# Mamba loop on one core: the order of ScalarE's queue within a tile, and one semaphore count for each square

## The chip, the cores and the metric

The kernel runs on one core of a Trainium2 chip. The metric is device time in microseconds (us) from one launch. Before the change three runs took 1242.48, 1243.62 and 1245.89 us; the median is 1243.62.

## What is computed

The reference is a layer of three blocks on x of shape (4, 1024, 256), in f32: half a mixture of experts, a Mamba block, half a mixture of experts again.

```python
x = x + 0.5 * ffn(layernorm(x))          # 8 experts, top 2, hidden 512, relu squared
x = x + mamba(layernorm(x))
x = x + 0.5 * ffn(layernorm(x))

def mamba_block(x, ...):                 # inner 512, state 16, conv 4, 64 heads of 8
    xn = layernorm(x) * ln_w + ln_b
    u = xn @ W_in                        # z | x, B, C | dt
    dt = softplus(u[..., -64:] + dt_bias)
    xBC = silu(causal_depthwise_conv(xBC, conv_w) + conv_b)
    # h = h * exp(dt A) + dt * x B ;  y = h C        over the sequence
    y = y + Dp * xs
    g = y * silu(z)
    g = g * rsqrt(mean(g * g) + EPS) * rms_w
    return x + g @ W_out
```

## The kernel before

The three blocks run one after the other. The change lies in the Mamba block alone, in the loop that starts some 350 us into the span.

A tile is 128 rows: 32 time steps of each of the 4 batches. There are 32 tiles. Every engine has its own program, in which a loop over `i` issues the stages of several tiles in an order written out by hand; semaphores (`m_...`) tie the engines together, and each engine executes its own queue strictly in order. The loop is software pipelined: round `i` does the heart of tile `i`, the gate, output projection and finish of tile `i - 1`, the conv and silu of tile `i + 1`, and the norm and the projections of tile `i + 2`. `inside(k)` says whether tile `k` exists.

What each engine does in a round, as far as the change touches it:

- ScalarE (`mamba_act`): `sums` takes the exponentials `ee` (L1101) of the decay sums, `skipped` copies `yi`, `decays` takes the exponentials of the 32 x 32 decay matrices (L1107), then come `squares`, `turned_gate` and `gate_in` for the gate, `shifted` and `normed` (L1133) for the tile two ahead. `out_of_heads` (L1140) copies the result `y1` of the matmuls `intra` out of PSUM. `tanh_conv` (L1148) is the tanh of the silu. `steps` (L1153 to L1159) takes |v|, v, exp(-|v|) and four squares `sq` for the polynomial of log(1 + e). `channels_bc` copies the last three conv columns of the tile before (L1167, "taps"), then B and C out of PSUM with the last conv tap (L1170) and raw (L1172). `finish` (L1196) scales the output projection of tile `i - 1` into `xo`. `channels` (L1181, L1183) does for the 512 channels of x what `channels_bc` does for B and C. `spread_c` (L1190) copies the masked C, `cm`, to the other 64 partitions; `turned_b` (L1211) copies the transposed B, `bt`.
- VectorE (`mamba_dve`): `weighted` makes `dtxw` (L932) from `dtx` and `ee`, `carried` makes `yc` (L926), `faded` scales the state, `stats` and `norm` serve tile `i + 2`, `decays` multiplies the decay matrices (L947), `gate` (L954) makes G from `yi`, `conv` runs 15 multiply-adds (L886), then come `gate_in`, `silu` (L892), `masked` and `own_batch`, `steps` with the four Horner steps (L865) and the step sizes, `pairs` (`cb`, L909) and `stepped` (`dtx`, L914). Its `steps` waits once for `m_e`, which ScalarE raises after its fourth square. Each Horner step waits for the one before through a `Chain`.
- TensorE (`mamba_pe`): `sums` (L1271, L1274), `inter` (L1283), which needs `m_cm` of `spread_c`, `decays`, `state`, `gate_in`, `turned_gate`, `project_out` (L1326), `intra` (L1370), the projections (L1257), `turned_channels`, `pairs`, which needs `m_Ub` of `channels_bc`, and `skipped`.
- GpSimd (`mamba_pool`) issues accumulating DMAs and small powers: `add_carried` (L1017), `deviation` (L997), `rms` (L1002, L1007, which raises `m_rr`), `add_turned` (L1028, adds `turned_y` to `yi`; the gate waits for it), `add_out` (L1012, adds `xo` to X).
- SP (`mamba_sync`) issues the other DMAs: `y1` to DRAM in the layout `turned_y` (L1074), `dtx` into the block diagonal `bd` (L1065), the loads of the experts' results.

Of the kernel before, what the change touches and what calls it, by code (L numbers as in the profile page):

```python
# [10 lines left out]
ACT = mybir.ActivationFunctionType  # L11
# [16 lines left out]
DI, DS_, DC, NH = 512, 16, 4, 64  # L28
# [17 lines left out]
LOG1P = ((0.4144192636013031, -0.962152361869812, 0.0742628201842308),  # L46
         (0.45970457792282104, -0.6549577116966248, 0.5710303783416748),
         (0.5534895062446594, -0.04552553594112396, 0.9979274272918701),
         (0.6860160827636719, 0.692435622215271, 0.5205329060554504))
# [40 lines left out]
def build(nc, a, out):  # L90
    with ExitStack() as ctx:
        def sb(name, shape, dt=F32):
            return ctx.enter_context(nc.sbuf_tensor(name, shape, dt))

        def sem(name):
            return ctx.enter_context(nc.semaphore(name))
# [116 lines left out]
        bias = sb("bias", [1, 3 * NH], mybir.dt.bfloat16)  # L213
# [5 lines left out]
        e_ = sb("e_", [P, NH])  # L219
        sq = sb("sq", [P, len(LOG1P) * NH])  # L220
        centre = sb("centre", [P, len(LOG1P)])
# [19 lines left out]
        def S(name):  # L241
            if name not in s:
                s[name] = sem(name)
            return s[name]
# [533 lines left out]
        def vc(i, j=0, n=None):  # L778
            return vec[:, V_OFF[i] + j:V_OFF[i] + j + (n or V_W[i])]
# [8 lines left out]
        def taps(p, lo, n):  # L788
            return U[p][:, :].rearrange("p (j b t) -> p j b t", b=B, t=QT + DC - 1)[:, :, :, lo:lo + n]
# [7 lines left out]
        def after(eng, name, count):  # L797

            if count > 0:
                eng.wait_ge(S(name), count)  # L800

        def inside(k):
            return 0 <= k < NT
# [12 lines left out]
        def mamba_dve(dve):  # L816
# [43 lines left out]
            def steps(k):  # L860
                p = k % 2
                cb_.at(k)
                dve.wait_ge(S("m_e"), k + 1)
                for n, (_, _, c) in enumerate(LOG1P):
                    cb_.link(dve.scalar_tensor_tensor(out=q_[:, :], in0=sq[:, n * NH:(n + 1) * NH], scalar=c,  # L865
                                                      in1=q_[:, :] if n else e_[:, :], op0=ALU.add, op1=ALU.mult))
                cb_.link(dve.scalar_tensor_tensor(out=dt_[p][:, :], in0=v_[:, :], scalar=0.0, in1=q_[:, :], op0=ALU.max, op1=ALU.add))
                cb_.link(dve.scalar_tensor_tensor(out=a_[:, :], in0=dt_[p][:, :], scalar=DOWN, in1=negA[:, :],
                                                  op0=ALU.mult, op1=ALU.mult))
                cb_.link(dve.tensor_scalar(a_[:, :], a_[:, :], CLAMP * DOWN, ASCALE / DOWN, ALU.max, ALU.mult))  # L870
                high, rest = a16[p][:, 0:NH], a16[p][:, NH:2 * NH]
                dve.tensor_copy(high, a_[:, :]).then_inc(S("m_a"), 1)
                dve.wait_ge(S("m_a"), 2 * k + 1)
                dve.tensor_tensor(rest, a_[:, :], high, ALU.subtract).then_inc(S("m_a"), 1)
                cb_.done()
# [80 lines left out]
            for i in range(FIRST, LAST):  # L956
# [25 lines left out]
                if inside(i + 2):  # L982
                    steps(i + 2)
# [102 lines left out]
        def mamba_act(act):  # L1086
# [11 lines left out]
            def sums(k):  # L1098
                act.wait_ge(S("m_ep"), k + 1)
                after(act, "m_Hd", k)  # L1100
                act.activation(ee[:, :], sums_ps, ACT.Exp, scale=1.0 / ASCALE).then_inc(S("m_ee"), 1)  # L1101

            def decays(k, g):
                act.wait_ge(S("m_Lp"), 4 * k + g + 1)
                if g == 0:
                    after(act, "m_intra", k)
                act.activation(by_heads(g), banks[5 - g % 2][:, :].rearrange("p (t h) -> p h t", h=NH), ACT.Exp, scale=1.0 / ASCALE)\  # L1107
                    .then_inc(S("m_L"), 1)
# [20 lines left out]
            def normed(k):  # L1129
                act.wait_ge(S("m_xT"), k + 1)  # L1130
                after(act, "m_z", k - 1)
                for c in range(KD):
                    m = act.activation(xnT[k % 2][:, c * P:(c + 1) * P], banks[0][:, c * P:(c + 1) * P], ACT.Identity,  # L1133
                                       scale=vc(V_LNW, c, 1), bias=vc(V_LNB, c, 1))
                m.then_inc(S("m_xnT"), 1)
# [14 lines left out]
            def steps(k):  # L1150
                act.wait_ge(S("m_dtp"), k + 1)
                after(act, "m_a", 2 * k)
                act.activation(vabs[:, :], v_ps, ACT.Abs).then_inc(S("m_abs"), 1)  # L1153
                act.activation(v_[:, :], v_ps, ACT.Copy).then_inc(S("m_v"), 1)
                act.wait_ge(S("m_abs"), 2 * k + 1)
                act.activation(e_[:, :], vabs[:, :], ACT.Exp, scale=-1.0).then_inc(S("m_abs"), 1)
                act.wait_ge(S("m_abs"), 2 * k + 2)
                for n, (c, _, _) in enumerate(LOG1P):
                    m = act.activation(sq[:, n * NH:(n + 1) * NH], e_[:, :], ACT.Square, scale=c, bias=centre[:, n:n + 1])  # L1159
                m.then_inc(S("m_e"), 1)  # L1160

            def channels_bc(k):
                p = k % 2
                act.wait_ge(S("m_U"), k) if k else act.wait_ge(S("m_zeroed"), 1)
                after(act, "m_Ub", k)
                after(act, "m_tap", (k - 1) * NTAP)
                act.activation(taps(p, 0, DC - 1), taps(1 - p, QT, DC - 1), ACT.Copy)  # L1167
                act.wait_ge(S("m_bcp"), k + 1)
                after(act, "m_g", 2 * (k - 1))
                act.activation(cv[p][:, NB * P:], banks[2][:, 0:P], ACT.Identity, scale=vc(V_CW, NB * DC + DC - 1, 1),  # L1170
                               bias=vc(V_CB, NB, 1))
                act.activation(taps(p, DC - 1, QT)[:, NB], banks[2][:, 0:P].rearrange("p (b t) -> p b t", t=QT),  # L1172
                               ACT.Copy).then_inc(S("m_Ub"), 1)
# [12 lines left out]
            def spread_c(k):  # L1186
                act.wait_ge(S("m_g"), 2 * (k + 1))
                after(act, "m_inter", k - 1)
                n = B * DS_
                act.activation(cm[k % 2][n:2 * n, :], cm[k % 2][0:n, :], ACT.Copy).then_inc(S("m_cm"), 1)  # L1190

            def finish(k):
                act.wait_ge(S("m_o"), k + 1)
                act.wait_ge(S("m_rr"), k + 1)
                after(act, "m_xout", 16 * (k - 1))
                act.activation(xo[k % 2][:, :], banks[5][:, 0:D], ACT.Identity, scale=mss[:, 2:3]).then_inc(S("m_x"), 1)  # L1196

            def skipped(k):
                act.wait_ge(S("m_xdp"), k + 1)
                after(act, "m_G", k - 1)  # L1200
                act.activation(yi[k % 2][:, :], banks[3][:, :], ACT.Copy).then_inc(S("m_yd"), 1)

            def state(k):
                act.wait_ge(S("m_sp"), k + 1)
                after(act, "m_state", 16 * k)
                act.activation(hn[:, :], banks[7][:, 0:DI // 2], ACT.Copy).then_inc(S("m_hn"), 1)
# [6 lines left out]
            for i in range(FIRST, LAST):  # L1213
                if inside(i):
                    sums(i)
                    skipped(i)
                    decays(i, 0)
                    decays(i, 1)
                if inside(i + 4):
                    choices(i + 4)  # L1220
                if inside(i):
                    state(i)
                    decays(i, 2)
                    decays(i, 3)
                if inside(i - 1):
                    squares(i - 1)
                    turned_gate(i - 1)
                if inside(i):
                    gate_in(i)
                if inside(i + 2):  # L1230
                    shifted(i + 2)
                    normed(i + 2)
                if inside(i):
                    out_of_heads(i)
                if inside(i + 1):
                    tanh_conv(i + 1)
                if inside(i + 2):
                    steps(i + 2)
                    channels_bc(i + 2)
                if inside(i - 1):  # L1240
                    finish(i - 1)
                if inside(i + 2):
                    channels(i + 2)
                if inside(i + 1):
                    spread_c(i + 1)
                    turned_b(i + 1)

        def mamba_pe(pe):
# [291 lines left out]
```

## Time and profile before

| what | value |
|---|---|
| median of 3 runs | 1243.62 us |
| the profiled execution | 1245.17 us |
| its span, first to last instruction | 1243.4 us |
| TensorE busy (matmuls) | 964.6 us, 78% |
| VectorE busy | 917.6 us, 74% |
| ScalarE busy | 701.8 us, 56% |
| GpSimd busy | 526.0 us, 42% |
| Mamba loop, first to last `ee` | 367.40 to 870.39 us |

Busy shares are means over three blocks with different limits, so the table does not say what sets the loop. For this the waits and the timeline of a single tile are read: each line of the timeline has the start of a group, the time from its start to its end, and in brackets how long the engine was idle before it and who ended that. Instructions on one engine overlap a little, so that the distance from one start to the next is often less than the duration.

### The profile page before, as it was taken

What the parts mean: (1) busy time and instruction counts of PE and PEld (TensorE: products, weight loads), DVE (VectorE), ACT (ScalarE), POOL (GpSimd) and SP (SyncE); (2) the same over time, 40 slices, a digit from 0 to 9 for tenths busy, and PEclk for the clock granted to TensorE, in tenths of its full rate; (3) what the DMA queues carried; (4) which work ended last, traced back from release to release, by engine and by line L of the source; (5) the groups of instructions that cost most, each with busy time, mean ns of one, the idle gap of its engine ahead of it and who ended that gap; (6) DMA issues with size and microseconds to landing.
All of it is one profiled execution on the core that took longest, in us unless ns stands there. A gap on an engine that the chain in (4) does not pass through costs nothing.

```text
span 1243.4 us, 39924 instructions
## 1 busy us (share of the span) xinstructions
PE 964.6 (78%) x14296; PEld 824.2 (66%) x14296; DVE 917.6 (74%) x2881; ACT 701.8 (56%) x1708; POOL 526.0 (42%) x591
## 2 busy tenths in 40 slices
PE   3442799999568999899898999998565269999960
PEld 3441789898456777677676777776364259999860
DVE  4987466666458998899988999998487636666648
ACT  2332455565357887788787888876222136665530
POOL 2787233333323444444444444443258723333320
PEclk9999999999869999999999999999655579999995
DMA  9556344444335666666666666654312434444549
GB/s 235 183 187 209 77 102 96 101 100 100 107 67 103 116 120 112 114 116 117 117 117 118 116 113 116 118 91 88 58 63 90 133 76 101 103 101 96 100 113 357
DMA packets 193056, 147.49 MB, mean 119 GB/s; under 512 B 112544, under 2 KB 160672, under 8 KB 192736
## 3 DMA queue, kind: packets, MB, share of 16 engines
q0 software_dynamic: 40992, 70.23, 27.1%
q1 hardware_dynamic: 146112, 69.45, 23.5%
q10 hardware_dynamic: 5760, 5.26, 1.3%
q8 instruction: 119, 1.95, 0.7%
q14 instruction: 73, 0.60, 0.2%
HBM read 41.34 MB, written 51.35 MB: 75 GB/s over the span
## 4 chain that ended last, share of the span: by engine, by line
PE 24%; DVE 19%; SPq 18%; issue 14%; ACT 10%; DMA 8%; POOL 7%; DVEq 0%; ACTq 0%; POOLq 0%
SPq L619 10%; DVE cv L886 6%; POOL disp L568 6%; PE bank L683 5%; PE bank L669 5%; PE bank L1257 4%; SPq L621 4%; DVE arena L947 3%; DMA disp<-arena,sloti 3%; ACT cv L1181 2%; PE bank L1326 2%; SPq L602 2%; PE bank L1297 2%; DMA arena<-disp 2%; ACT sq L1159 1%
## 5 line engine op out<-in xcount | busy, mean ns | idle before, releaser
L669 PE MATMUL bank<-arena,weights 128*128 128x128 f16 x3408 | 218.9, 223 | 60.1 <-DMA arena<-disp 59.5
L628 POOL DMA_INDIRECT ychosen<-arena,didx x142 | 138.7, 977 | 270.7 <-DVE didx L734 240.5
L669 PEld LDWEIGHTS bank<-arena,weights 128*128 x3408 | 205.7, 99 | 67.5 <-issue 64.6
L742 DVE TENSOR_TENSOR arena<-arena 128x512 f32<-128x512 f32 x142 | 98.3, 692 | 156.0 <-ACT arena L704 155.8
L683 PE MATMUL bank<-weights,arena 128*128 x1704 | 208.6, 273 | 0.0
L704 ACT ACTIVATE arena<-bank 128x512 f32<-128x512 f32 x142 | 84.8, 597 | 191.6 <-PE bank L669 177.9
L683 PEld LDWEIGHTS bank<-weights,arena 128*128 128x128 f16 x1704 | 160.8, 98 | 16.3
L568 POOL DMA_INDIRECT disp<-arena,sloti x128 | 132.4, 1034 | 59.0 <-issue 34.9
L886 DVE SCALAR_TENSOR_TENSOR cv<-U,vec,cv 128x128 f32<-128x128 f32 x480 | 128.7, 345 | 0.0
L1028 POOL DMA_DIRECT2D yi<-turned_y x32 | 27.8, 868 | 188.0 <-DMA turned_y<-y 188.0
L747 DVE TENSOR_TENSOR arena<-arena 128x512 f16<-128x512 f32 x142 | 98.2, 692 | 5.2 <-DVE arena L742 0.4
L708 ACT ACTIVATE arena<-arena 128x512 f16<-128x512 f32 x142 | 89.5, 630 | 4.5
L510 PE MATMUL bank<-cst,arena 128*128 128x128 f32 x128 | 31.4, 427 | 71.6 <-DVE arena L340 67.9
L947 DVE TENSOR_TENSOR arena<-arena,cb 128x512 f32<-128x512 f32 x128 | 84.7, 684 | 0.6 <-ACT arena L1107 0.5
L1107 ACT ACTIVATE arena<-bank 128x512 f32<-128x512 f32 x128 | 69.7, 601 | 17.7 <-PE bank L1297 17.7
L1297 PEld LDWEIGHTS bank<-a,arena 128*128 128x128 f16 x2048 | 64.1, 99 | 23.5 <-ACT arena L1107 11.9
L1033 POOL DMA_DIRECT2D X<-yg x64 | 64.1, 1002 | 36.3 <-DMA X<-yg 26.2
L1326 PE MATMUL bank<-wo,arena 128*128 128x256 f32 x256 | 65.5, 400 | 14.3 <-ACT arena L1117 14.1
L510 PEld LDWEIGHTS bank<-cst,arena 128*128 128x128 f32 x128 | 25.4, 225 | 73.5 <-DVE arena L340 56.6
L477 ACT ACTIVATE arena<-arena 128x512 f16<-128x512 f32 x32 | 18.4, 621 | 97.5 <-DMA disp<-arena,sloti 97.5
L1297 PE MATMUL bank<-a,arena 128*128 128x64 f16 x2048 | 71.7, 195 | 0.0
L1257 PE MATMUL bank<-xnT,wx 128*128 128x128 f32 x512 | 65.6, 283 | 0.1
(171 smaller groups left out, 2103.1 us busy)
## 6 DMA issues: line engine op xcount, KB each, us to landing
arena<-in_w SPq DMA_DIRECT2D x16, 512.0 KB, 4.9
yg<-ychosen SPq DMA_DIRECT2D x32, 256.0 KB, 2.8
X<-yg POOLq DMA_DIRECT2D x64, 128.0 KB, 3.9
arena<-dtx SPq DMA_DIRECT2D x128, 64.0 KB, 3.3
yi<-yc POOLq DMA_DIRECT2D x32, 256.0 KB, 4.1
turned_y<-y SPq DMA_DIRECT2D x128, 64.0 KB, 1.8
yi<-turned_y POOLq DMA_DIRECT2D x32, 256.0 KB, 4.1
arena<-ychosen SPq DMA_DIRECT2D x32, 256.0 KB, 5.3
```

Of the source, the lines that this page charges most:

```text
L568: pool.indirect_dma_start(disp, bass.IndirectOffsetOnAxis(ap=sloti[p][:, 2 * j + x:2 * j + x + 1], axis=0), drow[p][:, j * ROW:(j + 1) * R ...
L619: sp.dma_start(xTh[t % XIN].rearrange("p (c t) -> p c t", t=P), disp[ds(at, P), 0:2 * D], transpose=True)\
L628: pool.indirect_dma_start(ychosen, bass.IndirectOffsetOnAxis(ap=didx[:, t % NIDX:t % NIDX + 1], axis=0), ysb[t % YB][:, :], None).then_inc ...
L669: mm = pe.matmul(o, chunk(where, 2 * ("hl".index(w) * WN + c * HID + m * P), P), v, start=c == 0 and n_ == 0, stop=c == KD - 1 and n_ == 2)
L683: mm = pe.matmul(o, x, chunk(where, 2 * ((2 + "hl".index(w)) * WN + c * D), D), start=c == 0 and n_ == 0, stop=c == KH - 1 and n_ == 2)
L742: dve.tensor_tensor(hq[t % 2][:, :], hr[t % 2][:, :], hr[t % 2][:, :], ALU.mult).then_inc(S("hq"), 1)
L747: dve.tensor_tensor(hl[t % HB][:, :], hq[t % 2][:, :], hh[t % HB][:, :], ALU.subtract).then_inc(S("hl"), 1)
L886: dve.scalar_tensor_tensor(out=o, in0=taps(p, c, QT)[:, j], scalar=vc(V_CW, j * DC + c, 1), in1=o, op0=ALU.mult, op1=ALU.add).then_inc(S(" ...
L947: dve.tensor_tensor(u, u, cb[k % 2][:, g * TG:(g + 1) * TG].unsqueeze(1).to_broadcast([P, NH, TG]), ALU.mult)\
L1257: m = pe.matmul(o, x if tokens_first else ww, ww if tokens_first else x, start=c == 0, stop=last and c == KD - 1)
L1297: m = pe.matmul(o, upto[:, t * P:(t + 1) * P], a16[p][:, n * NH:(n + 1) * NH], start=n == 0, stop=n == 1)
L1326: m = pe.matmul(banks[5][:, 0:D], GT[:, j * P:(j + 1) * P], wo[:, j * D:(j + 1) * D], start=j == 0, stop=j == NB - 1)
```

## The change

Four things move in ScalarE's queue. The copy of the last conv columns becomes a function of its own, `last_taps`, and goes ahead of `out_of_heads`, behind `normed`. `finish` goes there too. The four squares of `steps` become `factors` and go behind `channels_bc`. `spread_c` goes ahead of `channels`. Besides, each of the four squares now raises `m_e`, and VectorE waits for the count of the square that it needs next, ahead of each Horner step, where it waited once for all four.

```diff
@@ mamba_dve: steps
                 cb_.at(k)
-                dve.wait_ge(S("m_e"), k + 1)
                 for n, (_, _, c) in enumerate(LOG1P):
+                    dve.wait_ge(S("m_e"), len(LOG1P) * k + n + 1)
                     cb_.link(dve.scalar_tensor_tensor(out=q_[:, :], in0=sq[:, n * NH:(n + 1) * NH], scalar=c,
@@ mamba_act: steps, channels_bc
                 act.activation(e_[:, :], vabs[:, :], ACT.Exp, scale=-1.0).then_inc(S("m_abs"), 1)
+
+            def factors(k):
                 act.wait_ge(S("m_abs"), 2 * k + 2)
                 for n, (c, _, _) in enumerate(LOG1P):
-                    m = act.activation(sq[:, n * NH:(n + 1) * NH], e_[:, :], ACT.Square, scale=c, bias=centre[:, n:n + 1])
-                m.then_inc(S("m_e"), 1)
-
-            def channels_bc(k):
+                    act.activation(sq[:, n * NH:(n + 1) * NH], e_[:, :], ACT.Square, scale=c, bias=centre[:, n:n + 1])\
+                        .then_inc(S("m_e"), 1)
+
+            def last_taps(k):
                 p = k % 2
                 act.wait_ge(S("m_U"), k) if k else act.wait_ge(S("m_zeroed"), 1)
                 after(act, "m_Ub", k)
                 after(act, "m_tap", (k - 1) * NTAP)
                 act.activation(taps(p, 0, DC - 1), taps(1 - p, QT, DC - 1), ACT.Copy)
+
+            def channels_bc(k):
+                p = k % 2
                 act.wait_ge(S("m_bcp"), k + 1)
@@ mamba_act: the loop over i
                     normed(i + 2)
+                    last_taps(i + 2)
+                if inside(i - 1):
+                    finish(i - 1)
                 if inside(i):
                     out_of_heads(i)
                 if inside(i + 1):
@@
                     steps(i + 2)
                     channels_bc(i + 2)
-                if inside(i - 1):
-                    finish(i - 1)
+                    factors(i + 2)
+                if inside(i + 1):
+                    spread_c(i + 1)
                 if inside(i + 2):
                     channels(i + 2)
                 if inside(i + 1):
-                    spread_c(i + 1)
                     turned_b(i + 1)
```

## Rows read from the trace of the kernel before

**Rows 1.** Waits between 400.19 and 838.25: who waited for whom, us in total, times, longest.
```profile
DVE dtxw L932 <- ACT ee L1101: 12.5, 27, 0.6
```

**Rows 2.** Timeline of ScalarE over one regular tile: start, us, instruction.
```profile
578.57 0.30 ACT L1101 ACTIVATE ee<-bank 128x160 f32<-128x160 f32 x1
...
588.18 0.60 ACT L1140 ACTIVATE y<-bank 128x512 f32<-128x512 f32 x1 [1.70 <-PE bank L1370]
...
589.82 0.26 ACT L1156 ACTIVATE e_<-vabs 128x64 f32<-128x64 f32 x1
590.11 1.06 ACT L1159 ACTIVATE sq<-e_,centre 128x64 f32<-128x64 f32 x4
591.09 0.25 ACT L1167 ACTIVATE U<-U 128x60 f32<-128x60 f32 x1
591.24 0.44 ACT L1170 ACTIVATE cv<-bank,vec 128x128 f32<-128x128 f32 x1
...
591.74 0.46 ACT L1196 ACTIVATE arena<-bank,mss 128x256 f32<-128x256 f32 x1
592.09 1.50 ACT L1181 ACTIVATE cv<-bank,vec 128x128 f32<-128x128 f32 x4
...
594.11 0.31 ACT L1190 ACTIVATE cm<-cm 64x128 f32<-64x128 f32 x1
594.45 0.22 ACT L1211 ACTIVATE bt<-bank 128x64 f32<-128x64 f32 x1
594.57 0.30 ACT L1101 ACTIVATE ee<-bank 128x160 f32<-128x160 f32 x1
```

**Rows 3.** Timeline of VectorE, the same tile and the start of the next.
```profile
591.50 0.21 DVE L865 SCALAR_TENSOR_TENSOR q_<-sq,e_ 128x64 f32<-128x64 f32 x1
...
593.64 0.18 DVE L909 TENSOR_TENSOR cb<-bank,cst 128x32 f32<-128x32 f32 x1
593.74 0.68 DVE L914 TENSOR_TENSOR dtx<-bank,dt 128x512 f32<-128x512 f32 x1
594.90 0.69 DVE L932 TENSOR_TENSOR dtxw<-dtx,ee 128x512 f32<-128x512 f32 x1 [0.48 <-ACT ee L1101]
...
597.95 0.68 DVE L954 TENSOR_TENSOR G<-yi,gz 128x512 f32<-128x512 f32 x1
```

**Rows 4.** Timeline of TensorE, the same tile.
```profile
584.86 1.99 PE L1326 MATMUL bank<-wo,arena 128*128 128x256 f32 x8 [0.47 <-ACT arena L1117]
...
593.75 0.29 PE L1274 MATMUL bank<-a,cst 128*128 128x64 f16 x4
```

**Rows 5.** Timeline of GpSimd, the same tile; the page's DMA issues (KB, us to landing).
```profile
584.62 0.77 POOL L1007 TENSOR_TENSOR mss<-mss,mhalf 128x1 f32<-128x1 f32 x1 [0.21 <-POOL mss L1002]
...
592.28 0.86 POOL L1028 DMA_DIRECT2D yi<-turned_y  x1 [5.56 <-DMA turned_y<-y]
...
yi<-turned_y POOLq DMA_DIRECT2D x32, 256.0 KB, 4.1
```

**Rows 6.** VectorE in the first experts block; the view of line L395 over the span.
```profile
66.21 0.22 DVE L391 TENSOR_REDUCE slotf<-prod 128x8 f32<-128x64 f32 x1
66.47 0.17 DVE L395 COPY arena<-ixf 128x4 f32<-128x4 f32 x1
...
L395 DVE COPY arena<-ixf x16: 170/171/173, 32.3 to 984.1; 128x4 f32<-128x4 f32 x16
...
  DVE slotf L391: 0.2, 1
```

**Rows 7.** A tile in which TensorE was late: its sums, and VectorE after them.
```profile
610.16 0.29 PE L1274 MATMUL bank<-a,cst 128*128 128x64 f16 x4
...
611.04 0.69 DVE L932 TENSOR_TENSOR dtxw<-dtx,ee 128x512 f32<-128x512 f32 x1 [0.62 <-ACT ee L1101]
```

**Rows 8.** A tile in which GpSimd was late: its DMA, and the gate.
```profile
837.53 0.86 POOL L1028 DMA_DIRECT2D yi<-turned_y  x1 [7.54 <-DMA turned_y<-y]
...
841.64 0.68 DVE L954 TENSOR_TENSOR G<-yi,gz 128x512 f32<-128x512 f32 x1
```

## The prediction

> **What bounds the kernel now.** I read the page first, then the waits of the Mamba loop, then one regular tile on each engine, then tiles that are not regular. Only the Mamba loop is touched, and 32 tiles pass through it. The waits say that neither ScalarE nor VectorE sets the loop alone: VectorE stands idle for ScalarE's `ee` at L932 ahead of every tile, 12.5 us over 27 tiles, 0.46 each [rows 1]. A smaller pause of VectorE, ahead of the silu, waits for the tanh that follows its own conv, and the change does not touch it.
>
> A regular tile takes 594.57 - 578.57 = 16.00 us from one `ee` to the next [rows 2]. The ring behind it: `ee` releases `dtxw` on VectorE, VectorE works through to the end of the conv, the tanh follows on ScalarE, and ScalarE then works through its queue in order until the next `ee`. On VectorE `dtx` ends at 593.74 + 0.68 = 594.42 and `dtxw` starts at 594.90, 0.48 later [rows 3]. ScalarE, on its side, was idle for 1.70 us just before `out_of_heads` (L1140 at 588.18) [rows 2]. So the queue after the tanh holds work that a hole before it could have taken.
>
> **What is the bound without that wait.** `dtxw` reads `dtx`, so it needs the end of the instruction ahead of it. Such a hand-over costs 0.04: a reduce of 0.22 starts at 66.21 and its successor at 66.47 [rows 6]. `dtxw` could start at 594.42 + 0.04 = 594.46, and a regular tile can give at most 0.44 us.
>
> **The change, part by part.**
>
> *Last taps and finish, moved ahead of `out_of_heads`.* From start to next start the taps (L1167) take 0.15 (591.09 to 591.24) and finish (L1196) 0.35 (591.74 to 592.09) [rows 2]. Both leave the queue after the tanh: 0.50. In their new place the idle 1.70 covers them. The taps need nothing late: their source and the last use of their target lie a tile back. Finish needs the output projection, whose matmuls end at 584.86 + 1.99 = 586.85 [rows 4], and GpSimd's `m_rr`, at 584.62 + 0.77 = 585.39 [rows 5]. It runs from about 586.9 to 587.35, and `out_of_heads` starts at 588.18 as now: cost 0, with 0.8 us of cover left. Were the cover gone, `out_of_heads` would stand behind it, and the tanh and the store of y after that, so nearly each us would be one of the tile. Finish releases one DMA, GpSimd's `X += xo`, which stays queued behind `add_turned` (L1028 at 592.28) [rows 5] and starts when it did. Nothing on SP waits for finish.
>
> *B and C ahead of the squares.* The exponential starts at 589.82 and the squares 0.29 later, since they read its result [rows 2]. B and C do not, so L1170 can follow at about 0.12, as `ee` follows `bt` (594.45, 594.57): another 0.17 is hidden. B and C take 591.24 to 591.74, 0.50, the squares 590.11 to 591.09, 0.98. New order: exponential 589.82, B and C 589.95 to 590.45, squares to 591.43. `m_Ub` comes 1.3 us earlier for TensorE.
>
> *One count of `m_e` for each square.* VectorE's first Horner step starts at 591.50 [rows 3] and lasts 0.21, so the four need their squares at 591.50, 591.71, 591.92 and 592.13 at the earliest. The squares would end at about 590.8, 591.1, 591.3 and 591.55. None waits. New is a second wait ahead of three of the four steps. The trace has this very pattern: the copy at L395 waits for its predecessor and, in 14 of its 16 executions, for a DMA long done as well. The view counts one idle time before it, 0.2 us; the others start like the one shown, 0.26 after the reduce's start [rows 6]. A second wait so costs between 0 and some 0.2 us; I bound it by 0.16 above the usual hand-over. A gain is excluded, nothing being removed. I take 0, as 13 of 14 show; the upper end is 3 x 0.16 = 0.48 a tile. The Trainium skill bears on this ("Perfetto Trace Analysis", Identifying Dependency Chains): in front of an instruction that waits for several engines, separate semaphore instructions may be inserted for the further conditions. It gives no duration. If each cost what the one slow case of L395 did, the sum below would turn into a loss of about 5 us; by the other 13 it stays as it is, and so far the trace speaks for these.
>
> *Masked C ahead of the channels.* `spread_c` (L1190) starts at 594.11 and `bt` (L1211) 0.34 later; with the 0.15 by which it starts later than an overlapped instruction would (my estimate), it occupies 0.49 [rows 2]. It keeps that in its new place, 591.5 to 591.9, since VectorE has written its source before it goes on to the Horner steps at 591.50. The channels (L1181) then start at about 591.86 in place of 592.09; they read TensorE's projection, and where TensorE is late they start no earlier than now. Channels and the copy into U take the 2.02 from 592.09 to 594.11, so ScalarE is at `bt` by 593.88 and not at 594.45. `bt` waits for VectorE's `cb`, which ends at 593.64 + 0.18 = 593.82 [rows 3]: `bt` at 593.88, `ee` 0.12 later at 594.00. TensorE's `inter` no longer waits for `spread_c` either.
>
> *TensorE.* `ee` also needs the sums, which end at 593.75 + 0.29 = 594.04 [rows 4] even if TensorE gains nothing. So `ee` starts at 594.07 and ends at 594.37, and `dtxw` could start at 594.40. Each of the three conditions comes before VectorE's own 594.46. The wait is gone, VectorE is the bound at 15.56 a tile, with 0.06 to spare at worst, and what is late next is `dtx` itself.
>
> *Sum.* 12.5 us in 27 tiles and two further tiles at the same 0.46 are 13.4. The hand-over, 29 x 0.04, takes 1.2. In two tiles TensorE was late: there `ee` can start at 610.16 + 0.29 + 0.03 = 610.48, so `dtxw` at 610.82 against 611.04 [rows 7]. They give 0.22 and not 0.62 - 0.04 = 0.58, together 0.7 less. 11.5 are left.
>
> *The other ring.* The gate (L954) needs `yi += turned_y`. In the regular tile that DMA is issued at 592.28 and lands 4.1 later, 596.4 [rows 5]; the gate starts at 597.95 [rows 3]. Of this 1.5 us of cover 1.1 would remain. In some tiles the cover is gone: issued at 837.53, landing at 841.6, gate at 841.64 [rows 8]. There nothing can be won. I put it at 0.9 in all, for four or five tiles that lose 0.1 to 0.4 each (an estimate between 0, if one tile alone is so, and the first rival). Fill and drain of the loop wait for TensorE and DMAs: 0. The gain is 11.5 - 0.9 = 10.6. The profiled execution took 1245.17 (its span 1243.4), so it would take 1234.6; it lay 1.5 above the median of the three runs. On that median: 1243.6 - 10.6 = **1233.0**.
>
> **The rivals.**
>
> *The wait comes back in part* (0.22). 0.06 to spare is little, and the DMA ring may be tight in more tiles: from L1028 to the gate there are 597.95 - 592.28 = 5.67 us in the one tile and 4.11 in the other. If half of the tiles gave nothing, the gain would be 11.5 / 2 = 5.7 less the 0.7 of late tiles: 1243.6 - 5 = 1238.6.
>
> *It does nothing that can be measured* (0.10). `ee` stays late by 0.3 us or more, say because ScalarE's instructions lose 0.1 of overlap at each of the four new seams, or because the DMA ring binds in nearly all tiles. A gain of 0 to 3.5: 1241.5.
>
> *Slower by the second waits* (0.05). They would fall on VectorE, the new bound. At 0.16 each, 0.48 x 32 = 15.4 lost against 10.6 won: 1248.4. The sign turns at 0.11 each. For it speaks one slow case, against it the other 13.
>
> *Slower by finish ahead of `out_of_heads`* (0.03). From `m_rr` later than 588.18 - 0.46 = 587.72 every further us delays the tile; slower by 0.3% takes 14.3 / 30 = 0.5 us more, so `m_rr` 2.8 us later than it comes now, in every tile: 1247.3. The 585.39 speaks against it.
>
> *More than forecast* (0.05). The stalls of TensorE and GpSimd in irregular tiles fall out better in the new rhythm. With the hand-overs and the late tiles given back: 1243.6 - 13.4, and another 3 for stalls: 1227.
>
> **How the numbers follow.** The forecast has 0.55; its own range is 1230.5 to 1236. A measurement of this kernel tells about 0.3%, 3.7 us, from no change. Faster by more than that is below 1239.9: the forecast, more than forecast and most of the first rival, 0.80; within it 0.13; slower 0.07. The range for 8 times in 10 runs from 1228 to 1240.5: it takes in the first rival, and some stalls on the low side.
>
> **What would show each step.** `dtxw`'s wait for `ee` falls from 0.46 to under 0.1; a regular tile takes 15.5 to 15.6; `cm` is copied about 2.4 us ahead of `bt`; `bt` waits for `cb`; finish stands ahead of `out_of_heads`, which starts no later after the matmuls of `intra`; the Horner steps stay 0.24 to 0.26 apart. I am wrong if `dtxw` still waits 0.3 us, if the gate waits for `yi` in many tiles, or if the Horner steps spread out.

## The result and the profile after

The changed kernel takes 1233.46 us (median of four runs, 1227.12 to 1233.83) against 1243.72 us (four runs): a ratio of 0.9905, 95% interval 0.9875 to 0.9934. 1233.0 was forecast. The ratios in this document are the estimates that belong to the intervals beside them; they are not the quotients of the two medians (0.9917 here). All numbers are of runs in the faster of two states of the program; a single run, of one_count, was in the slower one (1716.39 us, at a granted TensorE clock of 0.584) and is counted nowhere.

The waits of VectorE in the loop of the changed kernel come first (who waited for whom, us in total, times, longest; between 382 and 840 us, 29 tiles). The lines of code behind L1156 have moved a little: finish is now L1201, `channels` L1186, `spread_c` L1195, `bt` L1216.

```profile
DVE th L892 <- ACT th L1148: 7.4, 29, 0.9
DVE xn L855 <- POOL ma L997: 1.9, 2, 1.3
DVE G L954 <- DMA yi<-turned_y: 0.8, 2, 0.6
DVE dtxw L932 <- DVE dtx L914: 0.5, 1, 0.5
```

The wait for `ee` [rows 1] is gone from the list. The view of L932 over the whole span has it twice, 2.1 us, in the first and the last tile. What is left are the pause ahead of the silu, the gate's wait for its DMA, which now shows, and one pause of 0.46 in a single tile, whose `dtxw` starts at 526.73 although `dtx` and `ee` had ended at 526.27 and 526.18. The second trace of the changed kernel has it in the same tile; it was not followed up.

ScalarE over one regular tile, the answer to [rows 2]:

```profile
573.43 0.30 ACT L1101 ACTIVATE ee<-bank 128x160 f32<-128x160 f32 x1
...
581.38 0.27 ACT L1169 ACTIVATE U<-U 128x60 f32<-128x60 f32 x1
581.91 0.47 ACT L1201 ACTIVATE arena<-bank,mss 128x256 f32<-128x256 f32 x1 [0.26 <-PE bank L1334]
583.20 0.60 ACT L1140 ACTIVATE y<-bank 128x512 f32<-128x512 f32 x1 [0.81 <-PE bank L1378]
583.97 0.74 ACT L1148 ACTIVATE th<-cv 128x640 f32<-128x640 f32 x1 [0.17 <-DVE cv L886]
...
584.85 0.26 ACT L1156 ACTIVATE e_<-vabs 128x64 f32<-128x64 f32 x1
585.01 0.44 ACT L1175 ACTIVATE cv<-bank,vec 128x128 f32<-128x128 f32 x1
585.35 0.27 ACT L1177 ACTIVATE U<-bank 128x128 f32<-128x128 f32 x1
585.50 1.06 ACT L1161 ACTIVATE sq<-e_,centre 128x64 f32<-128x64 f32 x4
586.59 0.31 ACT L1195 ACTIVATE cm<-cm 64x128 f32<-64x128 f32 x1
586.92 1.50 ACT L1186 ACTIVATE cv<-bank,vec 128x128 f32<-128x128 f32 x4
...
588.95 0.22 ACT L1216 ACTIVATE bt<-bank 128x64 f32<-128x64 f32 x1
589.07 0.30 ACT L1101 ACTIVATE ee<-bank 128x160 f32<-128x160 f32 x1
```

Taps and finish stand in the hole. Finish waits 0.26 us for the output projection, 0.81 us of the hole remain, and `out_of_heads` still waits for TensorE's `intra`, not for finish. B and C start 0.16 after the exponential. From tanh to `ee` it is 589.07 - 583.97 = 5.10 us; before it was 5.63 (tanh at 588.94).

VectorE, at the end of the same tile [rows 3]:

```profile
586.52 0.21 DVE L865 SCALAR_TENSOR_TENSOR q_<-sq,e_ 128x64 f32<-128x64 f32 x1
586.76 0.75 DVE L865 SCALAR_TENSOR_TENSOR q_<-sq,q_ 128x64 f32<-128x64 f32 x3
587.54 0.23 DVE L867 SCALAR_TENSOR_TENSOR dt<-v_,q_ 128x64 f32<-128x64 f32 x1
...
588.67 0.18 DVE L909 TENSOR_TENSOR cb<-bank,cst 128x32 f32<-128x32 f32 x1
588.77 0.68 DVE L914 TENSOR_TENSOR dtx<-bank,dt 128x512 f32<-128x512 f32 x1
589.55 0.69 DVE L932 TENSOR_TENSOR dtxw<-dtx,ee 128x512 f32<-128x512 f32 x1
```

The four Horner steps and their successor start 0.24 to 0.27 apart, as before the change (591.50, 591.74, 592.52). A second wait costs them nothing. `dtxw` starts 589.55 - (588.77 + 0.68) = 0.10 after the end of `dtx` (0.10 to 0.11 in 29 of the 32 tiles), and no longer 0.48. The tile takes 15.64 us.

The edge of the loop changed as well. Two windows of the kernel before and two of the one after, from one `ee` to the next in the first tiles, to within 0.05 us (the columns are us, then busy us of TensorE's matmuls, its weight loads, VectorE, ScalarE and GpSimd, each with the instructions, then the granted TensorE clock as a share of 2.4 GHz, the DMA engines' share and GB/s). Before:

```profile
367.40:383.76 16.36, 13.70 (x258) 10.39 (x258) 14.17 (x45) 11.57 (x33) 5.03 (x6) 0.93 0.57 105
383.76:400.19 16.43, 15.09 (x270) 11.77 (x270) 14.87 (x46) 13.02 (x36) 6.68 (x9) 0.96 0.48 91
```

After:

```profile
367.40:382.85 15.45, 13.12 (x260) 9.76 (x260) 13.78 (x45) 11.44 (x32) 5.03 (x6) 1.00 0.58 106
382.85:398.50 15.65, 14.18 (x270) 11.28 (x266) 14.79 (x47) 13.27 (x37) 6.27 (x9) 1.00 0.53 101
```

From `ee` to `ee` 1.6 us were won in these two tiles. The sum had 0.2 for them: 0 for the edge of the loop, and 0.22 for the tile whose `dtxw` starts at 400.52, one of its two late tiles. At the end of the first tile, TensorE before:

```profile
380.94 0.38 PE L1389 MATMUL bank<-cmc,bm 64*128 64x32 f32 x2 [0.84 <-ACT U L1172]
381.33 1.84 PE L1395 MATMUL bank<-arena,th 128*128 128x128 f32 x8
```

And after:

```profile
380.53 0.38 PE L1397 MATMUL bank<-cmc,bm 64*128 64x32 f32 x2 [0.46 <-DVE cmc L904]
380.93 1.16 PE L1403 MATMUL bank<-arena,th 128*128 128x128 f32 x8
```

Before, TensorE waited 0.84 us for `m_Ub`, and the eight matmuls behind it took 1.84 us in place of the 1.16 of a regular tile: the granted clock between 381.3 and 383.2 was 0.58 of 2.4 GHz, so for most of that stretch the lower of its two levels, 1.2 GHz. After, it waited 0.46, now for `cmc` and no longer for `m_Ub`, and kept 2.4 GHz.

From the first `ee` to the last the loop takes 857.20 - 367.37 = 489.8 us, against 503.0. That is 13.2 less, while the medians differ by 10.3. The profiled execution of the changed kernel (1227.12 us) was the fastest of its four. Of the 18.1 us between the spans (1243.4 and 1225.3) 4.9 lie behind the last `ee`: 1.7 up to GpSimd's first instruction of the next block (L558), where the Mamba loop drains, and 3.2 behind that, in stages that the change does not touch.

### The profile page after: what moved, and what is told of

Its sections match the earlier page's. It is cut to its first block, busy times and chain, and to the rows that moved or that the text cites. A ratio compares the mean times of both kernels' runs of the same rounds, so it can differ in the third digit from the quotient of the medians.

```text
span 1225.3 us, 40020 instructions
## 1 busy us (share of the span) xinstructions
PE 958.2 (78%) x14296; PEld 822.7 (67%) x14296; DVE 918.0 (75%) x2881; ACT 710.5 (58%) x1708; POOL 530.0 (43%) x591
## 4 chain that ended last, share of the span: by engine, by line
DVE 32%; PE 23%; issue 14%; SPq 12%; POOL 10%; DMA 7%; ACT 3%; DVEq 0%; POOLq 0%; ACTq 0%
PE bank L669 10%; PE bank L683 10%; DVE cv L886 8%; POOL disp L568 7%; SPq L619 6%; DVE arena L947 4%; SPq L621 2%; DVE q_ L865 2%; DVE th L892 2%; ACT th L1148 2%; DVE yc L926 2%; PE bank L1265 1%; DMA yi<-turned_y 1%; DVE dtx L914 1%; DVE X L775 1%
```

## The experiments

Ten kernels were run, one of them the changed kernel itself once more. Those named together shared a chip and its runs of the kernel before; chips differ by some us, so ratios compare across them and medians only within a group. "The regular tile" is the distance from one `ee` to the next in tiles in which nothing is late. The first four answer which part of the change did it.

**front_only.** The kernel before, the taps taken out of `channels_bc` as `last_taps`, with

```diff
                     normed(i + 2)
+                    last_taps(i + 2)
+                if inside(i - 1):
+                    finish(i - 1)
                 if inside(i):
                     out_of_heads(i)
...
                     channels_bc(i + 2)
-                if inside(i - 1):
-                    finish(i - 1)
```

> The kernel before with only the last conv columns and finish moved ahead of out_of_heads. Theory (ScalarE's queue after the tanh sets ee): the queue is 0.50 us shorter, ee starts about 594.07 in place of 594.57, VectorE's wait for ee at dtxw is gone and a regular tile takes 15.6 us in place of 16.0, as with the whole change; only the edge tiles of the loop keep their slow TensorE clock, since m_Ub comes no earlier: 1234 to 1236 us. Rival (TensorE's waits for m_Ub and m_cm held the ring): both stay, so less than 3 us is gained, 1241 or more.

1241.53 us against 1250.91 on this chip: 0.9908 (0.9886 to 0.9931). That is 9.4 us less, where 8 to 10 were expected. The regular tile is 15.64, the loop 491.5 us. VectorE's waits in its loop:

```profile
DVE th L892 <- ACT th L1148: 7.4, 27, 0.7
DVE xn L855 <- POOL ma L997: 1.9, 2, 1.3
DVE dtxw L932 <- ACT ee L1101: 1.2, 3, 0.5
DVE G L954 <- DMA yi<-turned_y: 0.8, 3, 0.3
```

Two instructions moved by one place in a queue give what the whole change gives, within what can be told apart. Where the wait is not quite gone there is little room: in three tiles `ee` is late by up to 0.5. Against expectation the edge kept TensorE's clock: the wait for `m_Ub` at the end of the first tile was 0.69 us in place of 0.84, the clock stayed at full, and the first tile too was short (15.50). The second took 16.13.

**bc_only.** The kernel before with

```diff
                     steps(i + 2)
                     channels_bc(i + 2)
+                    factors(i + 2)
                 if inside(i - 1):
                     finish(i - 1)
```

where `factors` holds the four squares taken out of `steps`, each raising `m_e`, and VectorE waits for each count.

> The kernel before with only the squares moved behind B and C and one count of m_e for each. Theory: ScalarE hides 0.17 us behind the exponential, so ee comes 0.17 earlier and dtxw still waits 0.25 to 0.3; a regular tile takes 15.83; m_Ub is 1.2 us earlier, which keeps TensorE's clock up in the first and the last tiles for about 2 us more: 1236 to 1239 us. Rival (TensorE's wait for m_Ub held the ring): tile near 15.6, 1233. Rival (a second wait costs 0.16): slower than that by up to 15 us.

1247.12 against 1250.91: 0.9971 (0.9944 to 0.9997). The regular tile is 15.86. VectorE's wait for `ee`, over 28 tiles:

```profile
DVE dtxw L932 <- ACT ee L1101: 9.1, 28, 0.5
```

0.33 us each in place of 0.46: this part is worth 0.13 to 0.14 a tile by itself, and its `m_Ub`, over 1 us earlier, did not bring more: the medians fell by 3.8 us, where I had expected 5 to 8. The rival in which TensorE's wait for `m_Ub` held the ring is out.

**spread_only.** The kernel before with

```diff
+                if inside(i + 1):
+                    spread_c(i + 1)
                 if inside(i + 2):
                     channels(i + 2)
                 if inside(i + 1):
-                    spread_c(i + 1)
                     turned_b(i + 1)
```

> The kernel before with only the copy of the masked C moved ahead of the channels. Theory: ScalarE has the same work ahead of ee, so dtxw waits 0.46 as before, although TensorE's inter starts 0.4 us earlier: 1243 to 1244.5 us, tile 16.0. Rival (TensorE's inter held the ring): 1237 or less.

1251.76 against 1250.91: 0.9991 (0.9971 to 1.001), the regular tile 16.00, the wait for `ee` still there (11.6 us in 27 tiles):

```profile
DVE dtxw L932 <- ACT ee L1101: 11.6, 27, 0.6
```

TensorE's `inter` now starts 0.56 us ahead of `ee` (0.05 in the kernel before), and nobody profits.

**one_count.** The changed kernel with

```diff
-                for n, (_, _, c) in enumerate(LOG1P):
-                    dve.wait_ge(S("m_e"), len(LOG1P) * k + n + 1)
+                dve.wait_ge(S("m_e"), k + 1)
+                for n, (_, _, c) in enumerate(LOG1P):
...
-                        .then_inc(S("m_e"), 1)
+                m.then_inc(S("m_e"), 1)
```

> The changed kernel, but m_e is again raised once, after the fourth square, and VectorE waits once. In the trace of the changed kernel the fourth square ends 0.04 us after the first Horner step starts (586.56 and 586.52). Theory (second waits cost nothing): the first step starts 0.05 to 0.1 later in each tile, which on VectorE, now the bound, is 1.5 to 3 us more: 1235 to 1236.5. Rival (each second wait costs up to 0.16): 3 of them go, which gives back up to 0.48 a tile: faster than 1230.

1242.58 against 1250.91: 0.9913 (0.9888 to 0.9938). The medians cannot tell it from the other versions, the trace can: the first Horner step starts 0.36 after the reduce before it, where it was 0.29, and the regular tile is 15.71 to 15.79 in place of 15.63. It is so in every tile: 0.35 to 0.37 against 0.29 to 0.31.

```profile
574.38 0.37 DVE L904 TENSOR_REDUCE cmc<-cm 64x32 f32<-64x128 f32 x1
574.74 0.22 DVE L865 SCALAR_TENSOR_TENSOR q_<-sq,e_ 128x64 f32<-128x64 f32 x1
```

So the count for each square is what makes the move of the squares free of cost. Its second waits cost nothing: from the first Horner step to `dt` it is 1.02 us in the changed kernel, 1.02 in the kernel before, and 1.04 here, without them. The part of the 0.1 beyond these 0.07 and 0.02 I did not follow up.

The next four, again together, ask about the 0.11 between `dtx` and `dtxw`.

**after_again.** The changed kernel, unaltered.

> The changed kernel once more, unchanged, beside the others. The profiled execution of the changed kernel took 1227.12 us and its four timed runs about 1233.5. Theory: the regular tile is 15.63 us again and the loop, from the first to the last ee, 490 to 492 us; what varies by some us lies outside the loop and in its first and last tiles. Ratio 0.989 to 0.993. Rival: the regular tile itself differs from execution to execution.

1234.63 against 1246.97: 0.9898 (0.9875 to 0.9921). The regular tile is 15.63 to 15.65, the loop 492.95. The profiled execution (1238.41) was this time the slowest of its six, with 743.7 us outside the loop, against 735.5 in the first one. The gate waited three times, 1.6 us in all. Its last tile took 16.39 and not 15.01. The last tile of the first trace and of this one:

```profile
842.19:857.20 15.01, 11.01 (x239) 8.08 (x237) 12.20 (x31) 7.26 (x17) 4.16 (x7) 1.00 0.48 90
847.83:864.22 16.39, 12.46 (x241) 9.25 (x237) 12.11 (x31) 7.27 (x18) 4.36 (x7) 0.89 0.49 84
```

The work is the same, the granted clock is not: 1.00 and 0.89. In all twelve traces TensorE waits 2.23 or 2.24 us for the silu in this tile; behind that wait the clock stayed at 1.00 in three (last tile 14.95 to 15.15), and the tile had 0.94 in two (15.62 and 15.79) and 0.86 to 0.90 in six, the kernel before among them (16.21 to 16.57; the twelfth, of inter_before_skip, took 14.50 at 0.91 in another order of TensorE's work). The same kernel shows both, so the 1.2 us won there in the first trace are luck. What decides it no run shows.

**dtx_wait_first.** The changed kernel with

```diff
             def weighted(k):
-                dve.wait_ge(S("m_ee"), k + 1)
                 dve.wait_ge(S("m_dtx"), k + 1)
+                dve.wait_ge(S("m_ee"), k + 1)
```

> The changed kernel with the two waits of weighted in the other order: first m_dtx, then m_ee. In the changed kernel dtxw starts 0.11 us after the end of dtx, where other steps start 0.03 to 0.04 after their predecessor. Theory: of two waits the first written stands on the instruction and the second on a separate semaphore instruction ahead of it; the separate one costs about 0.07 when it is the one that is released last. With the order turned, dtxw starts 0.04 to 0.06 after dtx: tile 15.57, 2 us less than the changed kernel. Rival (0.11 belongs to this pair of instructions): tile 15.63, no difference.

1230.65 against 1246.97: 0.9871 (0.9848 to 0.9894).

```profile
635.23 0.68 DVE L914 TENSOR_TENSOR dtx<-bank,dt 128x512 f32<-128x512 f32 x1
635.94 0.69 DVE L932 TENSOR_TENSOR dtxw<-dtx,ee 128x512 f32<-128x512 f32 x1
```

`dtxw` starts 0.71 after the start of `dtx`, 0.03 after its end; in the changed kernel it was 0.78, 0.10 to 0.11 after the end, and the regular tile shrinks to 15.56 to 15.58. Reading this distance over the loop, I find 0.78 or 0.79 in 29 of 32 tiles of after_again and 0.71 to 0.76 in 29 of 32 here. The order of writing is what the 0.07 hung on. The medians lie 4 us apart, more than 29 x 0.07 = 2; what the other 2 are is not shown. In the two profiled executions the last tile (14.95 against 16.39) again differs by the clock.

**chain_wait_last.** The changed kernel with the two waits ahead of the Horner steps turned round:

```diff
                     dve.wait_ge(S("m_e"), len(LOG1P) * k + n + 1)
-                    cb_.link(dve.scalar_tensor_tensor(out=q_[:, :], in0=sq[:, n * NH:(n + 1) * NH], scalar=c,
+                    if n:
+                        dve.wait_ge(S("m_chain_b"), cb_.base + n)
+                    dve.scalar_tensor_tensor(out=q_[:, :], in0=sq[:, n * NH:(n + 1) * NH], scalar=c,
...
+                        .then_inc(S("m_chain_b"), 1)
```

(`link` waits for a step right behind it, ahead of the next round's `m_e`.)

> The changed kernel with the two waits ahead of the second, third and fourth Horner step in the other order: m_e first, the step before second. Theory as for the other order of waits: now the wait that is released last is on the separate instruction, in three steps a tile. They start 0.31 apart in place of 0.24, the tile takes 15.84, and the kernel is 6 to 7 us slower than the changed one. Rival (a second wait costs nothing however it is written): 0.24 apart, no difference.

1241.05 against 1246.97: 0.9961 (0.9942 to 0.998), 6.4 us slower than the changed kernel beside it. The regular tile is 15.83 to 15.86.

```profile
606.34 0.21 DVE L867 SCALAR_TENSOR_TENSOR q_<-sq,e_ 128x64 f32<-128x64 f32 x1
606.65 0.88 DVE L867 SCALAR_TENSOR_TENSOR q_<-sq,q_ 128x64 f32<-128x64 f32 x3
607.57 0.23 DVE L872 SCALAR_TENSOR_TENSOR dt<-v_,q_ 128x64 f32<-128x64 f32 x1
```

Three steps now start 0.31 to 0.33 after their predecessor (0.24 to 0.27 in the changed kernel), and `dt`, without an `m_e` ahead of it, still 0.26. From the first step to `dt` it is 1.23 against 1.02: 3 x 0.07 = 0.21 a tile, 6.7 us in 32 tiles. So the rival "slower by the second waits" has a true core. A second wait costs nothing where it is written behind the one that is released last, and 0.07 where it is written ahead of it. Written that way, the change would have lost half of its gain (6.4 of the 12.3 us between the medians of this group).

**ee_and_yc_first.** The changed kernel with

```diff
@@ mamba_dve: the loop over i
-                    weighted(i)
                     carried(i)
+                    weighted(i)
@@ mamba_act: the loop over i
                     sums(i)
+                    turned_b(i)
                     skipped(i)
...
                     channels(i + 2)
-                if inside(i + 1):
-                    turned_b(i + 1)
```

> The changed kernel with yc ahead of dtxw on VectorE, and ee ahead of bt on ScalarE. Then no step of VectorE has to wait for the end of dtx: yc starts 0.60 after the start of dtx, where dtxw started 0.79 after it, if ee is there in time, and without the wait for bt it ends about 0.3 us earlier. Theory (VectorE's own chain is the bound): a regular tile takes 15.44 us, some 5 us less in all than the changed kernel, ratio to the kernel before 0.986 to 0.988. Rival (the DMA ring through turned_y, yi and the gate is as tight as that): the gate waits in many tiles and little is gained.

1230.44 against 1246.97: 0.9864 (0.9841 to 0.9886). The regular tile is 15.51, not 15.44. The end of the tile, TensorE and VectorE:

```profile
603.91 0.70 PE L1290 MATMUL bank<-Hs,cm 64*128 64x256 f32 x4
604.02 0.68 DVE L914 TENSOR_TENSOR dtx<-bank,dt 128x512 f32<-128x512 f32 x1
604.71 0.69 DVE L926 TENSOR_TENSOR yc<-bank,ee 128x512 f32<-128x512 f32 x1
```

`yc` starts 0.69 after `dtx` and not 0.60: it waits for `inter`, which ends at 604.61, and that wait is written second. TensorE is now late at this place. The gate waits in four tiles ahead of the last, 2.5 us in all, so the rival has a small part.

Two more kernels, run together, follow this up.

**inter_wait_first.** ee_and_yc_first with

```diff
             def carried(k):
-                after(dve, "m_car", 16 * k)
                 dve.wait_ge(S("m_inter"), k + 1)
                 dve.wait_ge(S("m_ee"), k + 1)
+                after(dve, "m_car", 16 * k)
```

> The version with ee and yc first, and m_inter written as the first of the three waits of carried. There yc starts 0.10 after the last matmul of inter (604.61 and 604.71), on a wait that stands on the separate semaphore instruction. Theory: on the instruction itself it costs 0.03 to 0.04, yc starts 0.06 earlier, the tile takes 15.45 in place of 15.51, 2 us less in all. Rival (some other thing than the order costs 0.1): tile 15.51.

1233.74 against 1249.33: 0.9869 (0.9841 to 0.9897). The regular tile is 15.45 to 15.46, as expected.

```profile
604.66 0.70 PE L1290 MATMUL bank<-Hs,cm 64*128 64x256 f32 x4
605.41 0.69 DVE L926 TENSOR_TENSOR yc<-bank,ee 128x512 f32<-128x512 f32 x1
```

`yc` starts 0.05 after the end of `inter`, at 605.36; it was 0.10. Over the loop I find 0.04 to 0.09 in 30 of 32 tiles, against 0.10 to 0.12 in 30 of 32 of ee_and_yc_first. The whole kernel is not shown to be faster than that one.

**inter_before_skip.** The same with

```diff
@@ mamba_pe: the loop over i
                     sums(i)
                     inter(i)
+                    skipped(i)
                     decays(i, 0)
...
                     pairs(i + 1)
-                    skipped(i + 1)
```

> The same, and on TensorE the matmuls of skipped (1.1 us) moved behind sums and inter, so that inter is ready a us before VectorE asks for it. Theory (VectorE's own chain is the bound, nothing else is late): yc starts 0.60 after the start of dtx, tile 15.43 to 15.45, no pause at yc in late tiles either: 1 to 3 us less than the version before it. Rival (with inter early, ee at the end of ScalarE's queue is as late as it was): tile 15.5. Rival (the ring through yi and the gate has become the bound): pauses at the gate grow, and the gain is lost.

1232.42 against 1249.33: 0.9861 (0.9834 to 0.9889). The median tile is 15.48 us (15.69 and 15.75 in the two traces of the changed kernel), and the loop takes 482.3 us, 7.6 less than the better of those two. Against inter_wait_first, whose median tile is 15.46, no gain is shown: the loop is 2.7 us shorter, but the drain behind the last `ee`, up to the next block (L558 on GpSimd), 2.6 longer, at a granted clock of 0.76 against 0.84 over its first 20 us. From the first `ee` to the next block both take 511.1. `yc` now follows `dtx` by 0.60, but the other ring shows in the same tile:

```profile
616.36 0.68 DVE L914 TENSOR_TENSOR dtx<-bank,dt 128x512 f32<-128x512 f32 x1
616.96 0.68 DVE L926 TENSOR_TENSOR yc<-bank,ee 128x512 f32<-128x512 f32 x1
617.55 0.68 DVE L932 TENSOR_TENSOR dtxw<-dtx,ee 128x512 f32<-128x512 f32 x1
620.47 0.69 DVE L954 TENSOR_TENSOR G<-yi,gz 128x512 f32<-128x512 f32 x1 [0.38 <-DMA yi<-turned_y]
```

The gate waits in 3 of 31 tiles, 1.5 us in all. The ratio is the lowest of all, but its interval overlaps with those of dtx_wait_first, ee_and_yc_first and inter_wait_first; each beats the kernel before clearly, but their order among themselves is not shown. Against the changed kernel the traces say more, one for each. From the first `ee` to the next block it takes 515.3 and 519.9 us, the kernel before 530.1; dtx_wait_first takes 515.0 and ee_and_yc_first 515.9, which is within that spread, and the last two 511.1, which is below it.

## Why the prediction was right, point by point

- *The ring through `ee` and the hole ahead of `out_of_heads`.* Right. The wait of 0.46 is gone, and front_only shows that filling the hole suffices by itself.
- *Taps and finish cost nothing in their new place.* Right: `out_of_heads` waits for `intra` as before, with 0.81 us left (0.8 forecast).
- *B and C ahead of the squares hide 0.17.* bc_only measured 0.13 to 0.14 a tile. In the whole change this is spare time; it is not needed.
- *Second waits cost 0.* Right for the way they are written, which was luck: the prediction did not see that the order matters. chain_wait_last shows 0.07 each for the other order. The bound of 0.16 was not reached.
- *`spread_c` gives nothing.* Right: spread_only is 0.9991.
- *The hand-over of 0.04.* This term was mis-sized. The sum took the next bound to be the end of `dtx` plus 0.04, a tile of 15.56. It was 0.11 and 15.63, because the wait for `dtx` is written second in `weighted`; with the order turned, the 0.04 and the 15.56 appeared. 29 x 0.07 makes 2.0 us less gain than the sum had.
- *`ee` 0.06 in time.* In the tile shown `ee` ends at 589.37, 0.08 ahead of the end of `dtx` at 589.45. `bt` started at 588.95, 0.10 after the end of `cb`, where I had 0.03 to 0.06.
- *Fill and drain: 0.* Mis-sized the other way. The first two tiles gained 1.6 us in place of 0.2. The kernel before and spread_only, which wait 0.84 us for `m_Ub` there, have 16.36 and 16.43, and 16.19 and 16.50, and granted clocks of 0.93 to 0.96. All others wait 0.69 or less and have 1.00 in both tiles: bc_only 15.52 and 16.19, front_only 15.50 and 16.13. That the shorter wait kept the clock up is argued from these twelve traces; no run changed the clock alone.
- *The other ring, 0.9 us.* In the first trace of the changed kernel the gate waited 0.8 us in two tiles and 0.65 in the last but one; in the second 1.6 in three. These are waits; how much of them lengthened the loop was not measured, so the 0.9 is neither confirmed nor refuted.

These errors nearly cancel: 10.6, less 2.0 for the hand-over and plus 1.4 for the first two tiles, is 10.0. The loop gained 13.2 in one profiled execution (with 1.2 of luck in the last tile) and 503.0 - 492.95 = 10.0 in the other, the medians 10.3. Of the kernel before there is a single trace. Part of the close hit at 1233.0 is therefore chance. Not settled is what makes the time outside the loop differ by up to 12 us (735.5 to 747.5 us in these traces, from several chips); no experiment here touched it.

## What to carry to other kernels

Read a steady loop as a ring: find the wait that closes it, and look at the engine waited for, for a hole earlier in the same round. Work that is already possible in the hole shortens the round, but only until the next engine's own chain binds (here 0.50 us moved and 0.37 a tile won); a change that shortens a queue beyond that, or that makes another engine's input early, moves nothing. Then size the next bound down to the hand-over between instructions, since it caps the gain.

## What was not expected of the hardware

- Two waits ahead of one instruction differ by their order in the source: with the one that is released last written first, a VectorE step starts 0.03 to 0.05 us after its release, otherwise 0.10 to 0.11. Shown on `dtxw` (0.78 and 0.72 from start to start), on the Horner steps (1.02 and 1.23 over four of them) and on `yc` (0.10 and 0.05 after `inter`). ScalarE's `bt`, whose wait for `cb` is written second, likewise starts 0.09 to 0.10 after its end in 31 of 32 tiles of the changed kernel; that was not tried the other way. The Trainium skill ("Perfetto Trace Analysis", Identifying Dependency Chains) says that, ahead of an instruction that waits for several engines, semaphore instructions with the further conditions may be inserted. The profile shows no such instructions, so which wait stands where is not shown; the runs fit with it, and add the price and that the wait written first is the cheap one.
- A wait of TensorE of 0.84 us at the start of the loop went with a granted clock of 0.93 and 0.96 in two tiles, and 16.4 us for each of them (spread_only: 0.95 in both, 16.19 and 16.50); with 0.69 or 0.46 the clock was 1.00. The two tiles together gained 0.9 us more than twice the 0.37 of a regular one.
- Behind one and the same wait of 2.23 us in the last tile the granted clock was 1.00 in one execution of the changed kernel and 0.89 in the other, and the tile 15.01 and 16.39 us. A difference of 1.4 us between two single executions can be this and nothing else.
